# A fused graph network on one core: softmax totals from local runs, the node pass reordered with two additions on POOL, raw rows gathered with the first slots

## The reference

```python
# gat: h = x @ Wg per head; a_s, a_d = sums of h * att_src, h * att_dst
logits = leaky_relu(a_s[src] + a_d[dst] + ew[:, None], 0.2)
m = segment_max(logits, dst); ex = exp(logits - m[dst])
alpha = ex / segment_sum(ex, dst)[dst]
y = mean over heads of segment_sum(alpha * h[src], dst) + bias
x = relu(x + layer_norm(y))          # three such layers, one self loop per node
# around it: x = relu(node_features @ W0 + b0) before the first layer,
# after each network: out = layer_norm(x_in + network(x_in)); then two GCNs and a SAGE network
```

## Time and profile before

| what | value |
|---|---|
| time before, median of 3 runs | 5651.83 us (5644.61 to 5657.78) |
| the profiled execution's own time | 5648.55 us |
| its span | 5646.7 us |
| busy share of the span | PE 75%, DVE 70%, ACT 62%, POOL 44% |
| packets of SP's queue | 50.6% of 16 engines' span |

### The profile page before, as it was taken

One profiled execution on the slowest core, in us unless ns is written; L12 is line 12 of the kernel. 1 busy time (PEld: TensorE's weight loads), 2 busy tenths in 40 slices (PEclk: granted clock), 3 DMA queues, 4 the chain that ended last, 5 costly groups with the idle time before them and its releaser, 6 DMA issues. The chain is left out here.

```text
span 5646.7 us, 108972 instructions
## 1 busy us (share of the span) xinstructions
PE 4247.3 (75%) x22666; PEld 2953.2 (52%) x22666; DVE 3979.2 (70%) x15056; ACT 3517.7 (62%) x11198; POOL 2496.2 (44%) x2510
## 2 busy tenths in 40 slices
PE   3777777767688759989499888759876768786664
PEld 2555555544466525566355566524365656675544
DVE  5777777777778777777777677789844868654433
ACT  1777777766577647778467677648833767522222
POOL 2555555520144212255222344201176767676777
PEclk9999999989899979999799999979999999998777
DMA  2445555549799737689467699736654656554332
GB/s 74 153 157 162 162 159 157 157 152 314 255 294 297 252 108 229 215 287 308 145 193 229 219 293 291 248 112 227 208 156 146 213 183 213 166 158 128 91 98 75
DMA packets 617508, 1084.53 MB, mean 192 GB/s; under 512 B 105692, under 2 KB 131806, under 8 KB 617384
## 3 DMA queue, kind: packets, MB, share of 16 engines
q1 hardware_dynamic: 541928, 957.57, 50.6%
q0 software_dynamic: 75456, 125.65, 9.4%
HBM read 620.55 MB, written 466.24 MB: 192 GB/s over the span
## 5 line engine op out<-in xcount | busy, mean ns | idle before, releaser
L2195 POOL DMA_INDIRECT got_c<-table,src_row x980 | 931.3, 950 | 379.1 <-issue 296.8
L1233 POOL DMA_INDIRECT src_got_s<-table,src_row x588 | 554.6, 943 | 942.5 <-DVE delta_s L1471 486.9
L1783 POOL TENSOR_TENSOR part_m<-part_m,half_sum_m 128x512 f32<-128x512 f32 x147 | 220.9, 1503 | 1114.3 <-DVE half_sum_m L1997 1114.3
L2220 PE MATMUL bank<-pick_c,got_c 128*128 128x128 f32 x1960 | 327.1, 319 | 396.7 <-DMA got_c<-table,src_row 349.9
L1792 PE MATMUL bank<-w_all,dt_m 128*128 128x512 f32 x1176 | 569.0, 601 | 21.4 <-DMA dt_m<-delta_t 19.9
L2220 PEld LDWEIGHTS bank<-pick_c,got_c 128*128 128x128 f32 x1960 | 282.2, 222 | 439.0 <-issue 311.5
L1385 ACT ACTIVATE z_s<-z_s,shift_s,dev_s 128x128 f32<-128x128 f32 x1176 | 482.7, 483 | 4.6 <-DVE shift_s L1504 1.9
L2319 ACT COPY agg_c<-bank 128x512 f32<-128x512 f32 x245 | 143.4, 585 | 517.6 <-DVE bank L1633 286.4
L713 PEld LDWEIGHTS bank<-w_mean,ht 128*128 128x128 f32 x2352 | 346.2, 212 | 164.2 <-issue 164.2
L686 POOL DMA_INDIRECT raw_half<-in_x_dram,dst_node x196 | 204.7, 1044 | 492.5 <-PE bank L744 373.2
L710 PE MATMUL bank<-bias,first_row 128*128 128x512 f32 x588 | 353.6, 686 | 59.1 <-DVE rows L838 30.1
(11 more groups left out here) (310 smaller groups left out, 11854.6 us busy)
## 6 DMA issues: line engine op xcount, KB each, us to landing
table<-rows SPq DMA_DIRECT2D x294, 256.0 KB, 3.8
x_s<-table SPq DMA_DIRECT2D x294, 256.0 KB
x_c<-table SPq DMA_DIRECT2D x245, 256.0 KB
table<-mid_s SPq DMA_DIRECT2D x196, 256.0 KB
table<-z_s SPq DMA_DIRECT2D x196, 256.0 KB
table<-z_c SPq DMA_DIRECT2D x196, 256.0 KB
own_rows_s<-table SPq DMA_DIRECT2D x147, 256.0 KB
pick_t_s<-picks_t SPq DMA_DIRECT2D x147, 256.0 KB
```

What stands on the lines that cost most here:

```text
L1233: nc.gpsimd.indirect_dma_start(out=src_got[r][:, g, :], out_offset=None, in_=tables[l].rows, in_offset=bass.IndirectOffsetOnAxis(ap=src_ro ...
L1783: nc.gpsimd.tensor_tensor(flat(part[r]), flat(part[r]), flat(half_sum[r]), ALU.add).then_inc(parts_added, 1)
L2195: nc.gpsimd.indirect_dma_start(out=got[r][:, g, :], out_offset=None, in_=t_in.rows, in_offset=bass.IndirectOffsetOnAxis(ap=src_row[:, t:t ...
L2220: ins = nc.tensor.matmul(b_sum[r][:, k * P:(k + 1) * P], got[b.slot][:, k, :], pick[r][:, k, :], start=k == 0, stop=sage, skip_group_check ...
```

## The change

- `softmax`: `segments` is replaced by `run_totals`. It scans forwards once, and then takes the maximum backwards of those partial results within the row, which spreads each run's total over the run; the ends of both directions go over PE in one tile of 36 columns, and two sets of four `scalar_tensor_tensor` bring in what neighbours pass. Self scores are spread by a maximum in place of a sum. POOL adds the edge weights, ACT adds the shift of the self scores, the maxima let the edge exponential start earlier, and the division becomes a reciprocal of 2 x 392 columns after the transposes.
- `edge_structure` makes the masks for it (`run`, `link`, `tail_bound`).
- `node_chain`: the additions of layers 0 and 1 go to POOL (`add_rows`), the first shift goes from ACT to DVE (`shift_first`), all step lists are written anew and two to three steps deeper; the rings stay rings of two. The gathers of raw rows leave this stage.
- `first_slots`: POOL gathers the four groups of a batch straight from `x` into a ring of four, PE transposes them from there, and SP stores them; the load of `slot_x` goes.

```diff
@@ node_chain, SP
-                            b = at(2)
-                            if b:
-                                store_raw(b)
-                            b = at(4)
-                            if b:
+                                load_turned(b)
+                            b = at(5)
+                            if b:
+                                load_raw(b)
                                 store(0, b)
-                            b = at(5)
-                            if b:
                                 store(1, b)
+                            b = at(9)
+                            if b:
+                                store_last(b)
                             b = at(6)
                             if b:
...
                                 store(2, b)
...
+                        def load_raw(b):
+                            hold(sp, z_read, b.count(1, -1))
+                            sp.sem_inc(sp_pace, 1)
+                            sp.dma_start(flat(x0[b.half]), batch_rows(io["x"], b.batch())).then_inc(x0_in[b.half], 16)
@@ node_chain, POOL
+                        def add_rows(l, n):
                             r = n % 2
...
+                            pool.wait_ge(y_read[l], n + 1)
+                            pool.wait_ge(rows_made[l], n + 1)
+                            nc.gpsimd.tensor_tensor(flat(rows[l + 1][r]), flat(rows[l + 1][r]), flat(rows[l][r]),
+                                                    ALU.add).then_inc(summed[l], 1)
...
+                        for n in range(n_batches + 6):
+                            if n < n_batches:
+                                hold(pool, first_made, n - 2)
+                                if n == nb:
+                                    pool.wait_ge(placed, 16 * n_tiles)
+                                map_step(4 * n)
+                            if 6 <= n:
+                                add_rows(1, n - 6)
+                            if n < n_batches:
+                                map_step(4 * n + 2)
+                            if 4 <= n < n_batches + 4:
+                                add_rows(0, n - 4)
```

```diff
@@ first_slots
-                                hold(sp, x_turned, b.count(1, -1))
-                                sp.sem_inc(sp_pace, 1)
-                                sp.dma_start(x[r][:, :], batch_rows(raw.slots, b.batch())).then_inc(x_in[r], 16)
...
+                                sp.wait_ge(gathered[b.slot], b.ring4(64))
+                                sp.sem_inc(sp_pace, 1)
+                                sp.dma_start(batch_rows(raw.slots, b.batch()),
+                                             x[b.slot][:, :, :].rearrange("p g d -> p (g d)")).then_inc(raw_out[b.slot], 16)
...
+                        for b in range(nb):
+                            r = b % 4
+                            if b > 3:
+                                pool.wait_ge(x_turned, b - 3)
+                                pool.wait_ge(raw_out[r], 16 * (b // 4))
+                            for g in range(GB):
+                                t = b * GB + g
+                                nc.gpsimd.indirect_dma_start(
+                                    out=x[r][:, g, :], out_offset=None, in_=io["x"],
+                                    in_offset=bass.IndirectOffsetOnAxis(ap=dst_node[:, t:t + 1], axis=0)).then_inc(gathered[r], 16)
@@ run_totals
+            for h in range(HEADS):
+                ins = nc.vector.tensor_tensor_scan(seg_f[:, h, :], within[:, 0, :], val[:, h, :], neutral, *ops)
+            ch.step(ins)
+            nc.vector.tensor_copy(ends[:, 0:HEADS], seg_f[:, :, ROW - 1])
+            for h in range(HEADS):
+                ins = nc.vector.tensor_tensor_scan(seg_b[:, h, back], pen[:, 1, back], seg_f[:, h, back], -FAR, ALU.add, ALU.max)
+            ch.step(ins)
...
+            ch.step(nc.vector.tensor_copy(joined[:, :], bank[1][0:rq, 0:36]))
+            for d, source in ((0, seg_b), (1, seg_f)):
+                for h in range(HEADS):
+                    ins = nc.vector.scalar_tensor_tensor(seg_f[:, h, :], carry_mask[:, d, :], joined[:, 32 * d + h:32 * d + h + 1],
+                                                         source[:, h, :], *ops)
+                ch.step(ins)
```

More of the change, by code:

```diff
@@ L767, in turn_out, with relu_first, first_rows @@
                             nc.scalar.copy(flat(ht[l][b.half]), b_t[l][:, :]).then_inc(ht_made[l], 1)
-                        def step(at):
+                        def relu_first(b):
+                            act.wait_ge(first_made, b.count(1, 1))
+                            hold(act, ht_made[0], b.count(1, 0))
+                            nc.scalar.activation(hidden[:, :], b_x[:, :], ACT.Relu, bias=b_first[:, 0:1]).then_inc(hidden_made, 1)
+                        def first_rows(b):
+                            r = b.half
+                            act.wait_ge(first_turned, b.count(1, 1))
+                            hold(act, stored[0][r], b.ring(16, -16))
+                            hold(act, summed[0], b.count(1, -1))
+                            nc.scalar.copy(flat(rows[0][r]), b_rows[:, :]).then_inc(rows_made[0], 1)
@@ new lines, in last_deviation, with normalise @@
+                        def last_deviation(b):
+                            act.wait_ge(z_stat, b.count(1, 1))
+                            nc.scalar.activation(dev[3][b.half][:, :], stat[b.half][:, :, 1], ACT.Sqrt,
+                                                 bias=eps[:, 0:1]).then_inc(z_dev, 1)
+                        def normalise(b):
+                            r = b.half
+                            act.wait_ge(z_scaled, b.count(1, 1))
+                            hold(act, out[r], b.ring(16, -16))
+                            for g in range(GB):
+                                ins = nc.scalar.activation(z_out[r][:, g, :], z[r][:, g, :], ACT.Identity,
+                                                           bias=shift[r][:, g:g + 1], scale=dev[3][r][:, g:g + 1])
+                            ins.then_inc(z_made, 1)
@@ L773, in step @@
-                                act.wait_ge(z_scaled, b.count(1, 1))
-                                hold(act, out[r], b.ring(16, -16))
-                                for g in range(GB):
-                                    ins = nc.scalar.activation(z_out[r][:, g, :], z[r][:, g, :], ACT.Identity,
-                                                               bias=shift[r][:, g:g + 1], scale=dev[3][r][:, g:g + 1])
-                                ins.then_inc(z_made, 1)
+                                turn_out(2, b)
@@ L815, in step @@
[L815 to L818 removed]
+                                last_deviation(b)
+                        skewed(act, n_batches, 8, step)
                     @block.vector
@@ new lines, in add_last, with residual @@
+                        def add_last(b):
+                            r = b.half
+                            dve.wait_ge(y_read[2], b.count(1, 1))
+                            dve.wait_ge(rows_made[2], b.count(1, 1))
+                            nc.vector.tensor_tensor(z[r][:, :, :], z[r][:, :, :], rows[2][r][:, :, :], ALU.add).then_inc(summed[2], 1)
+                        def residual(b):
+                            r = b.half
+                            dve.wait_ge(summed[2], b.count(1, 1))
+                            dve.wait_ge(x0_in[r], b.ring(16))
+                            nc.vector.scalar_tensor_tensor(z[r][:, :, :], z[r][:, :, :], 0.0, x0[r][:, :, :], ALU.max,
+                                                           ALU.add).then_inc(z_read, 1)
@@ new lines, in moments @@
+                        def moments(b):
+                            r = b.half
+                            dve.wait_ge(z_read, b.count(1, 1))
+                            for g in range(GB):
+                                ins = nc.vector.bn_stats(stat6[:, g, :], z[r][:, g, :])
+                            ins.then_inc(z_moments, 1)
+                            dve.wait_ge(z_moments, b.count(1, 1))
+                            dve.sem_inc(dve_pace, 1)
+                            for g in range(GB):
+                                ins = nc.vector.bn_aggr(stat[r][:, g, :], stat6[:, g, :])
+                            ins.then_inc(z_stat, 1)
@@ L893, in step @@
-                            b = at(0)
-                            if b:
-                                combine(0, b, rows[1][b.half])
-                        skewed(dve, n_batches, 4, step)
+                                moments(b)
+                        skewed(dve, n_batches, 8, step)
         def first_slots(w_first, b_first, beta_col):
@@ L1564, in _ @@
+                    @block.gpsimd
+                    def _(pool):
+                        pool.wait_ge(edge_in, 16)
+                        for h in range(HEADS):
+                            ins = nc.gpsimd.tensor_tensor(lr[:, h, :], lr[:, h, :], ew_rows[:, layer, :], ALU.add)
```

(11 more changed lines are left out.)

399 lines of the change are left out of this document (212 added, 187 removed).

## The result

The changed kernel takes 5560.85 us (median of 4 runs, 5558.32 to 5566.37); the kernel before took 5650.55 beside it (4 runs, 5644.61 to 5657.78). The ratio is 0.9841, 95% interval 0.9826 to 0.9857: 90 us less, where some 25 were forecast (22 by its sum, which started from the profiled execution, 3.3 under the median), and 11 us under the low end of the range. The profiled execution has a span of 5558.9 us, 87.8 under that of before.

What follows compares the result with a forecast made beforehand. Node pass was taken as bound by a chain of waits, first slots by transfers. Terms -5 + 0 + 64 - 85 + 4 = -22 against 5648.55 gave 5626.5, forecast as 5627 us, range 5572 to 5676.

Steps and rivals of the forecast that it cites:

- issue to release 3.89: Node pass: time from SP issuing the second row store until DVE's `scale 0` may start, taken as 3.89 us.
- the loop: Node pass: DVE's residual, SP's raw load and two stores, landing, `scale 0` to next residual; 11.65 us, taken as 11.45.
- Its DVE part: Node pass: DVE's instructions from `scale 0` to the end of the next residual, summed to 6.3 us per batch.
- Fill and drain: Node pass ends: step lists two steps deeper cost between 0 and +23 us; taken as 0.
- the sign of being wrong: Whole prediction: wrong if softmax gives under 60 us or the node pass moves by over 50.
- 5.9 us per batch: First slots: 4.2 us of DMA plus 1.27 for gathers, at a 0.92 share, gives 5.9 per batch, +64 us.
- Rival B: First slots: gathers cost only POOL's issue pace, +27 us in place of +64, total 5590; chance 0.2.
- Rival A: Node pass: store release nearer 2.9 than 3.89 us, loop 10.4, 108 us more gain, some 5520; chance 0.1.
- Rival C: Node pass: POOL's additions hold DVE, up to 1.26 us per batch, +123 us, total 5750; chance 0.13.
- Softmax: Three softmax layers: shorter scans, totals and division save 28.3 us per layer, -85 us in all.
- rival D: Softmax: sets of four cost 2.8 us, not 1.4, so 8 more per layer, total 5652; chance 0.05.
- edge_structure: Mask building before the node pass: two scans and some fifteen short operations on DVE's path, +4 us (3 to 6).

Runs made afterwards that it cites:

- stores first: Changed kernel with SP issuing the stores of rows 0 and rows 1 ahead of the raw row load: node pass 9.89 us per batch against 10.88, ratio to before 0.9779.

## Why the forecast was wrong

The forecast was a gain and it came; its size was over three times too small. Two steps failed in the same direction, together by 79 us, and a third took 9 back.

- **Node pass, "issue to release 3.89".** This term of the loop is the step that failed. The loop itself is right, with its releases, and stores first showed that it binds. But the term measured 3.39 (mean), 0.50 less. Of this, 0.12 is that 3.89 was read from one step of the kernel before, whose mean is 3.77. Up to 0.22 is that its queue held raw gathers that the change takes away, by the run of the old order without them. They had been costed by what waits for them ("They held nobody in the node pass"), not by what they stand in front of. The rest, 0.16 or more, stays open: the raw stores don't explain it (without them the release was no shorter), and a gather put back into the new order moved it by under 0.1. The lower bound had 0.5 for "fewer bytes queued" (11.0 per batch, -48 us). That size is what came, its reason only in part, and I took the middle.
- **Its DVE part** was 6.3 against 6.14 measured. The sum was then taken down from 11.65 to 11.45, with no term for it. With the measured terms it is 11.02, which is the period in the middle of the pass. The forecast set this period against 11.50, a mean with the quicker first batches in it; like with like it is 11.59 to 11.02, and 11.50 to 10.85.
- **Fill and drain**: taken at 0, measured 10 us at the end, inside the bounds of 0 to 23. The first batches gave back some 8: that is the part of 10.85 that lies under 11.02. The whole pass moved by 53, over the 50 that the forecast had named as the sign of being wrong.
- **First slots, "5.9 us per batch".** The gathers' bytes were priced at 206 GB/s from the earlier trace rows, another stage, with the engines at 92%. Here they moved at 270, which makes 4.2 + 0.262 / 270 x 1000 = 5.2 us of DMA per batch. Even that is too much: the engines were busy 0.96 of 5.04, 4.8 us, and the division by 0.92 that the forecast put on top came out as one by 0.96. So the transfers fitted under POOL's 5.04. Rival B's account (POOL's pace) is the one that the runs bear out. It gave +27; the stage gave +32.8. The rule of the Trainium skill that pieces of 512 B and more go at line rate (DMA: Bandwidth & Descriptors, Specifications) is not borne out here either: 270 against the 370 GB/s of the queue of large transfers (42.62 MB in 76.8% of 150 us).
- **Rival A**, the release at 2.9: it went half of the way from 3.89. **Rival C** had the mechanism and the wrong place. DVE is held when POOL's addition has started before it: its shift takes 1.49 us, 0.48 at its shortest. But it is the shift, in front of DVE's idle time, and not the instructions of the loop, so it cost nothing until the loop was broken; then it and the shift's own time were worth 1.07 us per batch. The forecast had put this shift at 0.4 to 0.7, as it is alone.
- **Softmax** gave 25.3 per layer, not 28.3. Its sets of four at 98x256 take 1.67, where 1.4 was estimated from one instruction of 98x1024 (rival D had 2.8); seven of them are 1.9 per layer. The first scans beside POOL's additions cost 1.4 more.
- **edge_structure** was right: +4.2 for +4.

The range failed because its low end, 55 under the forecast, had room for rival B (37) and less than half of the loop's bound (48). Both came whole, or nearly. Two independent terms with gains of 48 and 37 within their own bounds reach 5542 together.

## What to carry to other kernels

A transfer that is moved has two prices, one where it goes and one where it leaves: a release time read from a trace holds what stood in the queues beside it, so when traffic leaves a stage, the old value is an upper bound and not a forecast. Read such a time as a mean of many steps: single ones ran here from 2.78 to 4.68 us. A loop through a wait is best judged by its list order: here two stores issued ahead of one waiting load were worth 1.0 us of 10.9 per batch. And work shed by an engine that has idle time in front of a wait shows nothing until that wait is gone: the shift's 1.49 us gave 0 with it and 1.07 without.

## What the hardware showed that was not expected

- POOL's two-input addition and DVE hold each other, and the second to start is the one that is held: DVE's one-input shift takes 1.49 us inside POOL's addition and 0.47 ahead of it, its two-input addition 1.23 inside and 0.68 otherwise, POOL's addition 1.56 to 1.65 behind DVE's residual and 1.26 to 1.30 otherwise. A scan of 256 columns beside POOL's additions takes 1.14 (median) in place of 0.67. The trace of before had shown only POOL as loser, since POOL was second in the row shown. The exclusive lock that the Trainium skill describes (SBUF — State Buffer, SBUF: two separate sides) does hold DVE too, by who starts first.
- The time from issue to release of a 256 KB store follows what is queued ahead on its queue: 3.39 (mean) with 512 KB of load and store just in front of it, 2.62 with 384 KB. Not all that is queued counts alike: a 128 KB store taken out of the old order's queue, one place further ahead, left it at 3.68 after 3.55.
- Gathers of 64 KB come every 1.25 us on one chip, with POOL's issues as the bound, and every 1.85 us on another, with a third of the DMA engines' time idle. There a batch of first slots takes 7.54 us and not 5.25, so the changed kernel's gain is 1.6% on the first kind and 1.15% on the second.
